# Second attention of a two-layer cross-attention and expert kernel: the queries' addition moves from VectorE to GpSimd, both halves of the first normalisation come behind the first maximum, and the low half of the context waits for them

## The reference, cut to what matters

```python
q = Q @ Wq.T + bq ; k = K @ Wk.T + bk ; v = K @ Wv.T + bv   # Q: normalised rows, K: context
A = softmax(qh @ kh.T / 16)
O = concat_heads(qh + A @ vh)           # the queries are added to the output
O = layernorm(O, g0, b0)                # first normalisation
O = O + relu(O @ Wo.T + bo)
O = layernorm(O, g1, b1)                # second normalisation
x = x + O
```

## Time and profile before

| what | value |
|---|---|
| three runs | 1877.29, 1878.34, 1880.26 us, median 1878.34 |
| the profiled execution, own time | 1879.33 us |
| its span, first to last instruction | 1877.2 us |
| busy share PE / DVE / ACT / POOL | 85% / 57% / 43% / 43% |
| mean granted TensorE clock | 0.905 |

### The profile page before, as it was taken

The page is one execution under the profiler, slowest core; times in us unless marked ns, Lnnn a source line. Parts: engine busy times, 40 slices in busy tenths (PEclk is TensorE's granted clock), DMA queues, the critical chain, the costliest instruction groups (busy, mean ns, idle before and its releaser), DMA issues. The chain is left out here.

```text
span 1877.2 us, 48532 instructions
## 1 busy us (share of the span) xinstructions
PE 1602.5 (85%) x16482; PEld 1195.6 (64%) x16483; DVE 1070.6 (57%) x2269; ACT 806.9 (43%) x1574; POOL 816.0 (43%) x1127
## 2 busy tenths in 40 slices
PE   5999999999944999995999999999998329999667
PEld 4777777777732666664777777777777314444345
DVE  3666666666634222222677766776667466766445
ACT  3777777777730222222655455545555101111111
POOL 3666666666631111113555454545554113333363
PEclk8999999999976999997998888988889559999879
DMA  4112121111014111112112111211110203333464
GB/s 123 53 55 75 53 75 53 30 30 30 16 45 182 33 32 34 34 31 82 32 59 73 55 51 55 73 33 29 32 29 11 100 27 103 105 108 109 116 162 115
DMA packets 57879, 119.23 MB, mean 64 GB/s; under 512 B 12556, under 2 KB 30964, under 8 KB 54484
## 3 DMA queue, kind: packets, MB, share of 16 engines
q1 hardware_dynamic: 45348, 90.25, 14.7%
q0 software_dynamic: 12464, 28.08, 5.6%
HBM read 89.32 MB, written 28.97 MB: 63 GB/s over the span
## 5 line engine op out<-in xcount | busy, mean ns | idle before, releaser
L968 DVE TENSOR_REDUCE a_mx<-a_SM 100x2 bf16<-100x722 f32 x384 | 351.5, 915 | 198.7 <-PE a_SM L431 192.0
L706 ACT ACTIVATE a_Pr<-a_ST 120x1600 f32<-120x1600 f32 (+3 forms) x192 | 225.3, 1173 | 160.6 <-PE a_ST L463 159.8
L755 POOL TENSOR_TENSOR a_rstd<-a_ve,a_powers 100x1 f32<-100x1 f32 x192 | 114.3, 595 | 325.3 <-DVE a_ve L938 324.3
L431 PE MATMUL a_SM<-a_KT,a_QM 32*100 32x362 f32 x768 | 159.8, 412 | 60.3 <-DVE a_mx L968 55.7
L1705 PE MATMUL g_PH<-w,g_xT 128*128 x456 | 207.1, 597 | 0.0
L473 PE MATMUL a_M<-a_Pr,a_V 120*32 120x100 f32 (+3 forms) x4608 | 198.7, 270 | 0.0
L473 PEld LDWEIGHTS a_M<-a_Pr,a_V 120*32 120x32 f32 (+3 forms) x4608 | 155.0, 130 | 24.1 <-issue 14.3
L431 PEld LDWEIGHTS a_SM<-a_KT,a_QM 32*100 32x100 f32 x768 | 64.6, 164 | 120.8 <-DVE a_mx L968 92.2
L1705 PEld LDWEIGHTS g_PH<-w,g_xT 128*128 128x128 f32 x456 | 83.1, 192 | 83.6 <-issue 83.6
L361 PE MATMUL a_M<-a_ch,a_wkh 128*128 128x362 f32 x256 | 100.7, 393 | 29.1 <-POOL a_cl L823 28.7
L812 POOL TENSOR_TENSOR a_KL<-a_KF,a_KT 128x724 fp32r<-128x724 f32 x64 | 111.1, 1737 | 30.8 <-ACT a_KT L599 30.7
(11 more groups left out here) (198 smaller groups left out, 3714.0 us busy)
## 6 DMA issues: line engine op xcount, KB each, us to landing
w<-in_E_w SPq DMA_DIRECT2D x24, 1024.0 KB, 6.0
a_ct<-in_ctx SPq DMA_DIRECT2D x64, 362.0 KB, 3.1
gated_rows<-g_hs SPq DMA_DIRECT2D x57, 256.0 KB
keep_rows<-a_keep SPq DMA_DIRECT2D x64, 100.0 KB
tile_rows<-e_y SPq DMA_DIRECT2D x32, 128.0 KB, 1.7
b_rows<-in_E_b SPq DMA_DIRECT2D x1, 4096.0 KB
out<-g_y SPq DMA_DIRECT2D x32, 100.0 KB
X<-in_x SPq DMA_DIRECT2D x1, 2800.0 KB
```

Of the source, the lines that this page charges most:

```text
L431: last = nc.tensor.matmul(SM[0:LQ, half, 0:LKP], QM[b.p][rows, chunk, m, :], KT[b.p][rows, chunk, :], start=True, stop=True)
L706: nc.scalar.activation(Pr[0:n, s, :].rearrange("p (r q) -> p r q", r=GROUPS), ST[0:n, :, 0:PER * LQ], ACT.Exp, scale=SCALE).then_inc(exp_d ...
L755: nc.gpsimd.tensor_tensor(rstd[k][:], ve[k][:].to_broadcast([LQ, n]), powers[:, 0:n], ALU.pow).then_inc(rstd_ready[k], 1)
L968: V_.tensor_reduce(pair, SM[0:LQ, :, 0:LK], AX_X, ALU.max).then_inc(max_done, 1)
```

## The change

GpSimd takes over the addition `o += qtok` as the last thing of its step. DVE waits for it instead of doing it. `tail1a` and `tail1c` both stand behind max0. On GpSimd, power 1 goes ahead of the low keys, the low context waits for `o1_ready`, `residual1` goes ahead of power 0, the index copy of the gather and the low queries go ahead of power 3.

```diff
+            def queries_added(b):
+                pool.wait_ge(norm_read, b.count(1, 1))
+                pool.wait_ge(qtok_biased, b.count(1, 1))
+                nc.gpsimd.tensor_tensor(o[:], o[:], qtok[b.p][:], ALU.add).then_inc(qtok_used, 1)
+
+            def gather_rows(b):
                 if b.low >= 2:
                     pool.wait_ge(x2_done, b.count(1, -1))
                 wait_apart()
                 nc.gpsimd.tensor_copy(gidx[b.p][:], env["slots"][:, bass.ds(b.at, 1)]).then_inc(gidx_ready, 1)
+
+            def gather(b):
                 pool.wait_ge(gidx_ready, b.count(1, 1))
...
+                if tail and layer == 1:
+                    power(1, prev)
                 if fr:
                     low_parts(nxt)
-                if tail and layer == 1:
-                    power(1, prev)
                 if ahead and layer == 1:
+                    if tail:
+                        pool.wait_ge(o1_ready, prev.count(1, 1))
                     low_context(nxt2)
+                if ends:
+                    residual1(prev2)
                 if ahead:
                     power(0, nxt2)
-                if ends:
-                    residual1(prev2)
...
+                if ahead and layer == 1 and nxt2.low + 1 < NB:
+                    gather_rows(nxt2.plus(1))
+                if fr:
+                    masked_low(nxt)
                 if ends:
                     power(3, prev2)
-                if fr:
-                    masked_low(nxt)
...
                 if ahead and layer == 1 and nxt2.low + 1 < NB:
                     gather(nxt2.plus(1))
+                if back and layer == 1:
+                    queries_added(b)
...
-                dve.wait_ge(norm_read, b.count(1, 1))
                 if b.low == 0:
                     dve.wait_ge(rest_loaded, REST_LOADED)
-                dve.wait_ge(qtok_biased, b.count(1, 1))
-                V_.tensor_tensor(o[:], o[:], qtok[b.p][:], ALU.add).then_inc(qtok_used, 1)
                 dve.wait_ge(qtok_used, b.count(1, 1))
...
                     if tail and j == 0:
                         tail1a(prev)
-                    if tail and j == 1:
                         tail1c(prev)
```

More of the change, by code:

```diff
@@ L794, in query_bias @@
                 nc.gpsimd.tensor_tensor(qtok[b.p][:], qtok[b.p][:], bvb[:], ALU.add).then_inc(qtok_biased, 1)
-            def gather(b):
+            def queries_added(b):
[3 more added lines that the diff above has]
+            def gather_rows(b):
                 if b.low >= 2:
@@ L887, in step @@
                     gather(nxt2.plus(1))
+                if back and layer == 1:
+                    queries_added(b)
             if layer == 1:
-                gather(fixed(0))
-                gather(fixed(1))
+                for b in range(2):
+                    gather_rows(fixed(b))
+                    gather(fixed(b))
             nc.gpsimd.memset(powers[:, 0:1], -0.5)
```

## The result

The changed kernel takes 1786.98 us (median of 4 runs, 1784.52 to 1789.04) against 1877.82 us for the kernel before in the same session: the ratio is 0.9514, 95% interval 0.9497 to 0.953. The profiled span fell from 1877.2 to 1785.8 us, the mean granted clock rose from 0.905 to 0.934.

A forecast was written before the change was run, and what follows sets the result against it. TensorE bounds the kernel, with waits and a halved clock in even steps. From 1879.3 us, -76.8 (loop), -2.4 (peeled steps) and +0.3 (last tail) give 1800.4, as a median 1799.4; predicted 1799.5, range 1792 to 1828.

The forecast's parts named there:

- The mechanism: Even looped steps: DVE's addition beside GpSimd's keys delays max0; the 1.50 us gap before SM1 drops the clock; both go.
- The addition: On GpSimd at its step's end: about 0.73 us, ending T + 1.7 to 2.75, T being the start of L439.
- the sum for a looped step: Second attention's loop: odd step 15.53 us, even 15.63, a pair 31.16 instead of 37.56; 12 pairs give -76.8 us.
- The peeled steps: Four steps outside the loop lose their wait of about 0.6 us for L439: -2.4 us.
- The last tail: Last sequence's tail: nothing covers GpSimd's addition, 726 ns against DVE's 0.47 us: +0.3 us.
- The price of each part: `residual1` ahead of power 0 on GpSimd ends the L439 wait: -0.73 us on every odd step.
- The rule against: VectorE about twice as fast as GpSimd; the addition at plain price on the path in 32 steps: +10 us.
- The range: Whole kernel: 1792 to 1828 us; main case, chance 0.80, 1794 to 1813 from waits of 0 to 0.6 us a step.

The follow-up runs named there:

- run (d): Kernel before, with one added wait: GpSimd's low keys wait until DVE has added the queries. 1843.25 us, ratio 0.9813.
- the two runs with the gap made by hand: Changed kernel with two further maxima ahead of max0, in the loop's even or odd steps: 1856.74 us (0.9858) and 1855.01 us (0.9847).
- run (b): Kernel before, with only the addition to x (`residual1`) ahead of power 0 on GpSimd: 1794.45 us, ratio 0.9556.
- second session: Changed kernel and run (b) timed again on one chip against the kernel before: 1786.89 us (0.9499) and 1791.21 us (0.9515).
- Run (g): Changed kernel with the addition to x behind power 0 again: 1826.17 us, ratio 0.9701.
- (a): Kernel before, with only the queries' addition moved to the end of GpSimd's step: 1868.51 us, ratio 0.9945.
- (c): Kernel before, with only both normalisation halves behind max0, power 1 ahead of the low keys, the low context held until o1 is ready: 1839.57 us, 0.9792.
- run (f): Changed kernel with the queries' addition back on DVE: 1794.39 us, ratio 0.9531.
- run (e): Changed kernel without the low context's wait for `o1_ready`: 1860.32 us, ratio 0.9871.

## Why the prediction was right and where it was wrong

*The mechanism.* Right. DVE's addition stretched by the keys made max0 late (run d), the gap made the clock fall in whichever step it stood (the two runs with the gap made by hand), and both went. The looped steps are alike, 15.13 to 15.33 us, at a clock of 1.00. Which part of the change removes the gap is another matter, see the price of each part.

*The addition.* Right: 0.74 us for the forecast 0.73, its end at T + 1.75, at the low end of T + 1.7 to 2.75. Its meeting with `tail1b`'s last instruction cost 0.55 us, inside the bound of 0.73.

*The failed step: the sum for a looped step.* "Odd step: 16.16 - 0.73 + 0.1 = 15.53. Even step: ... 15.63." Measured 15.28 for both: 24 x 0.30 = 7.3 us of the 12.5 by which the span was missed (78.9 forecast, 91.4 measured). Put beside each other, an odd step by its L439 and SM starts and the rows of after:

```
              L439-SM0  SM0-SM1  SM1-SM2  SM2-SM3  SM3-L439   sum
before          4.50     1.42     2.08     3.93      4.23    16.16
after           4.65     1.42     1.94     3.82      3.45    15.28
(b) alone       4.53     1.42     2.06     3.94      3.36    15.31
```

The last row is the odd step of run (b) at 1121.75. I put SM2 at T + 8.00 plus a wait of 0.1 (0.2 in even steps), since both halves of the normalisation now stand ahead of max1. There is no such wait: SM2 is at T + 8.01, and from there to SM3, where PE transposes o1, it takes 0.11 less than before. In the odd step of before, `tail1a` was held beside the context, so max1 and o1 were late there too. DVE, `tail1a` and max1:

```profile
1129.07 1.13 DVE L1010 SCALAR_TENSOR_TENSOR a_o<-a_o,a_mv,a_g0b 100x256 f32<-100x256 f32 x1
1130.32 0.91 DVE L968 TENSOR_REDUCE a_mx<-a_SM 100x2 bf16<-100x722 f32 x1
```

I priced `tail1a` at 0.47 us in the new step and did not ask what it took in the old one, 1.13. From the start of `tail1a` to max1 it is 1.25 us there and 1.12 in the changed kernel, with both halves in it. And I took T + 8.00, where PE reached SM2, for the time at which PE is free; max1 ended just there (1131.23, SM2 at 1131.29). A start without a wait in brackets is not proof that an engine came there unhindered. Of the 0.25 us by which the odd step was missed, 0.09 is at SM2, 0.11 behind it, and 0.05 behind SM3 (0.78 gained for the 0.73 counted); the even step's further 0.1, for the branch, did not come either.

One thing went the other way: SM0 is 0.15 us later than in the odd step of before. ScalarE's copy of the keys' product and the value product of PE behind it, at T + 1.09 (T + 0.97 before):

```profile
1059.01 0.55 ACT L591 ACTIVATE a_KF<-a_M,a_bk 128x362 f32<-128x362 f32 x1
```

```profile
1059.61 0.38 PE L361 MATMUL a_M<-a_wvh,a_ch 128*120 128x256 f32 x1
```

The product starts 0.05 us behind the copy's end. The table so shows why the rest of the change is worth so little beside (b): it wins 0.24 us between SM1 and SM3 and loses 0.21 around L439.

*The peeled steps.* I counted 0.6 us of L439 wait in four of them, -2.4. Measured from the L439 of the first sequence to that of the last, 561.7 us became 472.3; of these 89.4 us the loop has 84.1 and the rest 5.3. The three steps behind the loop alone went from 48.05 to 44.06 us: two of them had the held `tail1a` as well (1.32 and 1.38 us), not only the wait. The first step was 1.3 us longer, 16.67 for 15.39; in the changed kernel's second session it took 15.66.

*The last tail.* Forecast +0.3, measured -0.45 from the last L439 to the end of the stage (34.46 to 34.01 us). GpSimd's addition runs beside `tail1b`, where DVE's stood behind it. The remaining 1.6 us came mostly in the stages behind the attention, where nothing was changed; their cause was not tried.

*The price of each part.* Here my account was incomplete. I gave `residual1` ahead of power 0 the 0.73 us of L439 alone, as the first term. Run (b) shows that it also carries DVE's addition from T + 3.04 to T + 2.19, while `a_KT` is ready at T + 2.51 instead of T + 2.84; the addition is no longer held, and with that go the gap and the fall of the clock. Alone it gives 85 us (89 in the second session). The prediction had given the removal of the gap to the addition's move to GpSimd. Run (g) shows a second route, by `kept` on ScalarE, which makes up 0.26 of the 0.56 us by which SM0 was later in the even step; in run (b) all of it is gone (SM0 at T + 4.51 in even steps). I used that number and did not ask for its cause. The other parts do not add up with it: alone they give 11 (a) and 39 us (c), and each leaves a hindrance that the rows above show: the context beside `tail1a` in (a), the late queries' product and the L439 wait in (c).

*The rule against.* GpSimd's addition costs 0.74 us for DVE's 0.43, and by run (f) it hardly matters on which of the two it is, with the rest in place. The Trainium skill's advice ("GPSIMD Engine Reference", Engine selection) would have kept it on VectorE. The longer time on GpSimd is there, 1.7 times DVE's; a loss of the kernel by it no run here shows.

*The range.* The low end was built from waits of 0 to 0.6 us added to a base step of 15.43, which itself held waits; no case below the base was allowed for. Nor do the prediction's own sums give its bounds exactly: no wait in any step comes to 1795.8, and 0.6 us in every step to 1810.2, where it says 1794 and 1813.

## What to carry to other kernels

Before making an engine's work cheaper, look for what starts it late: here the exchange of two calls on GpSimd, an engine busy 43% of the span, took DVE's addition out of a collision that three other parts of the change were built around. When a wait is taken away, the next one in the same queue shows, so price a part by undoing it with the rest of the change in place, and not only alone. And compare a stretch with the sum of its own work, not with its best instance, for that may be waiting too.

## What was not expected of the hardware

The length of one wait does not tell whether the clock falls. It stayed in all steps of run (d), with waits of 0.6 to 0.8 (one of 1.00), 0.33 and 0.25 to 0.5 us, and in two steps of run (e) with one of 1.30:

```profile
1284.73 0.41 PE L431 MATMUL a_SM<-a_KT,a_QM 32*100 32x362 f32 x2 [1.30 <-DVE a_mx L979]
```

It fell in all even steps of run (a), ten of them with about 0.7, 0.33 and 0.93 and two with only 0.33 and 0.63 or 0.80; in three steps of run (c) in which no wait passed 0.74; in one step of run (e) with 0.33 and 0.25 (at 1148.73); and in one of run (b) with 0.33 alone (the one of 16.86 us). What decides it is open. The falls also differ in price: that step of run (b) took 1.6 us more than its neighbours, those of run (c) 3.4 us.

The gather's issue waited 0.93 us behind the index copy right in front of it, and 0.19 us where the copy stands some instructions earlier, though the copy itself takes 0.18 to 0.4.
